# A decoder layer on one core: the routing in groups of 4, 4, 4, 2 and 2 tiles, entered earlier, rows stored by batch

## The reference

```
x = layernorm(x + attn(x))      # linear attention, 16 heads: relu(q), relu(k), kv = k^T v, gated
x = layernorm(x + xattn(x, ctx))
    # q from x, k and v from ctx [8, 256, 512]; 16 heads of 16 rows; softmax over 512 positions
x = layernorm(x + ffn(x))
    logits = x @ router_weight.T + router_bias            # 16 experts
    top_val, top_idx = top_k(logits, 4); top_val = softmax(top_val)
    gate, up = (x @ gate_up_proj[e] + bias)[::2], [1::2]  # gate <= 7, up in -7..7
    out = sum_e score[e] * (((up + 1) * gate * sigmoid(1.702 * gate)) @ down_proj[e] + down_bias[e])
```

## Time and profile before

| | us |
|---|---|
| median of 3 runs (lowest to highest) | 1608.12 (1604.43 to 1608.62) |
| the profiled execution | 1606.24 |
| its span | 1604.6 |
| its mean granted clock | 0.954 |

### The profile page before, as it was taken

The page is one execution under the profiler, slowest core; times in us unless marked ns, Lnnn a source line. Parts: engine busy times, 40 slices in busy tenths (PEclk is TensorE's granted clock), DMA queues, the critical chain, the costliest instruction groups (busy, mean ns, idle before and its releaser), DMA issues. The chain is left out here.

```text
span 1604.6 us, 29621 instructions
## 1 busy us (share of the span) xinstructions
PE 1454.8 (91%) x7542; PEld 1028.6 (64%) x7543; DVE 966.7 (60%) x1414; ACT 738.4 (46%) x1416; POOL 862.1 (54%) x704
## 2 busy tenths in 40 slices
PE   6999999699999999986749999999999999999991
PEld 5878887444444444431537787777777777877770
DVE  2324344778878888898635555555555555555554
ACT  4212222277788778764223444434344443444233
POOL 4425334555666765536146636656666666476221
PEclk9999999799999999998659999999999999999995
DMA  5201022554657556620375545656656566473336
GB/s 215 68 14 49 13 49 54 83 85 72 104 106 130 103 92 121 100 44 19 112 265 128 147 94 158 158 119 154 157 153 157 145 159 158 111 194 74 60 59 219
DMA packets 94741, 180.63 MB, mean 113 GB/s; under 512 B 19113, under 2 KB 21929, under 8 KB 94025
## 3 DMA queue, kind: packets, MB, share of 16 engines
q1 hardware_dynamic: 74968, 133.04, 32.7%
q0 software_dynamic: 18544, 46.13, 14.4%
q10 hardware_dynamic: 1152, 0.52, 0.2%
HBM read 116.32 MB, written 33.73 MB: 94 GB/s over the span
## 5 line engine op out<-in xcount | busy, mean ns | idle before, releaser
L934 DVE TENSOR_REDUCE stage<-ps_a 128x2 f32<-128x1024 f32 x256 | 300.1, 1217 | 70.4 <-PE ps_a L1264 69.8
L1984 POOL TENSOR_TENSOR we_split<-we_raw,we_split 128x512 f32 (+1 forms) x192 | 248.5, 1533 | 108.1 <-ACT we_split L1975 92.8
L734 ACT ACTIVATE probs<-ps_b 128x512 f32<-128x512 f32 x498 | 270.5, 595 | 50.3 <-PE ps_b L1279 44.1
L2288 PE MATMUL ps_y<-we_split,hT 128*128 x912 | 235.4, 407 | 6.0 <-DVE hT L2219 3.5
L2288 PE MATMUL ps_g<-we_split,xT 128*128 x912 | 230.7, 401 | 8.4 <-issue 5.6
L2288 PE MATMUL ps_u<-we_split,xT 128*128 x912 | 231.0, 402 | 0.0
L2288 PEld LDWEIGHTS ps_g<-we_split,xT 128*128 128x128 f32 x912 | 171.1, 190 | 60.4 <-issue 21.3
L2288 PEld LDWEIGHTS ps_y<-we_split,hT 128*128 128x128 f32 x912 | 168.1, 190 | 44.4 <-issue 9.0
L2288 PEld LDWEIGHTS ps_u<-we_split,xT 128*128 128x128 f32 x912 | 166.0, 189 | 34.4
L2087 POOL DMA_INDIRECT scratch_acc<-x_keep,to_rows x76 | 121.2, 1595 | 90.2 <-issue 54.0
L2077 POOL DMA_INDIRECT x_rows<-scratch_x,from_rows x79 | 78.6, 995 | 133.4 <-ACT from_rows L2147 107.7
(11 more groups left out here) (320 smaller groups left out, 2252.7 us busy)
## 6 DMA issues: line engine op xcount, KB each, us to landing
we_raw<-in_w_expert SPq DMA_DIRECT2D x192, 256.0 KB, 2.9
stack<-xT_raw SPq DMA_DIRECT2D x192, 128.0 KB, 5.5
...
scratch_acc<-x_keep SPq DMA_DIRECT2D x1, 4096.0 KB, 18.4
...
```

The lines of the kernel that those rows point to most:

```text
L734: nc.scalar.activation(probs[:, n % 3, h], src[:], ACT.Exp, scale=DH ** -0.5).then_inc(b_kept, 1)
L934: nc.vector.tensor_reduce(out[:, :, i, k % NC], ps_a[i][:], AX.X, ALU.max, negate=True).then_inc(a_kept[i], 1)
L1984: nc.gpsimd.tensor_tensor(lo, W["raw"][:, k, c], hi, ALU.subtract).then_inc(W["lo"], 1)
L2288: mm = nc.tensor.matmul(out[:], left[:, a, c], w[:, bass.ds(par, 1), k, b, c].squeeze(1), start=(n == 0), stop=(n == len(passes) - 1))
```

## The change

The groups are 4, 4, 4, 2 and 2 tiles; `LATE`, the one left for `route()`, has two. Group 0's top_experts, constants and chosen_experts stand in batch 6 at steps 7, 9 and 11. In the last batch stand top 1 (step 0), rank_slots 0 (step 3) and chosen 1 (step 6). Behind the loop VectorE's temporaries lie in ps_a0's second half (`temps_in_psum`), which leaves the ring one bank fewer; rank_slots copies chosen there first. TensorE ranks groups 0, 1, 2 at steps 1, 7, 15 and group 3 behind the last values, has both turns of batch 6 at step 13 and its logits at step 14. GpSimd marks 4 tiles ahead of finish_heads, then 4, then 6. The digits of a slot are compared as integers and two of the three comparisons are one instruction. x is stored to scratch_acc batch by batch behind the store to scratch_x. share_weights of 14 tiles and its store are last. In `route()` the experts' counts and tables are computed around the marks instead of behind them, GpSimd splits gate and up as soon as slots_made has come, the first product waits only for gate, and SP begins with expert 1 once three gathers have landed.

```diff
-                return {3: [("rank", 0)], 4: [("turn", 2 * b - 4)], 5: [("turn", 2 * b - 3), ("rank", 1)],
+                return {1: [("rank", 0)], 4: [("turn", 2 * b - 4)], 5: [("turn", 2 * b - 3)],
...
+                sp.dma_start(S["acc"][b * L:b * L + L, :].rearrange("(i p) d -> p i d", p=P),
+                             x[:, 2 * b:2 * b + 2, :]).then_inc(R["acc_stored"], 16)
...
-                if t == NT - 2:
-                    store_weights(sp, S, R, K["weights"], 0, 3)
+                sp.dma_start(S["acc"][t * P:t * P + P, :], x[:, t, :]).then_inc(R["acc_stored"], 16)
+            store_weights(sp, S, R, K, 0)
...
-                    for t in range(8):
+                    for t in range(4):
...
-            for t in range(8, 10):
-                mark_tile(nc.gpsimd, pool, R, K, t, in_tiles[t], of_tiles[t])
             pool.wait_ge(y2_moments, B - 1)
             nc.gpsimd.tensor_tensor(rstd2[:], mean_var2[:, :, 1], minus_half2[:], ALU.pow).then_inc(y2_rstd, 1)
             for o in range(2):
-                if o == 1:
-                    for t in range(10, EARLY_TILES):
-                        mark_tile(nc.gpsimd, pool, R, K, t, in_tiles[t], of_tiles[t])
+                for t in range(4, 8) if o == 0 else range(8, EARLY_TILES):
+                    if t == 12:
+                        pool.wait_ge(b_made, USE["exp", N - STEPS // 2 - 1, 3] + 1)
+                    mark_tile(nc.gpsimd, pool, R, K, t, in_tiles[t], of_tiles[t])
...
-                if b == B - 1 and s in (0, 2):
-                    if s == 0:
-                        dve.wait_ge(b_made, USE["exp", n - 1, 3] + 1)
-                        dve.wait_ge(b_kept, USE["qk", b, 3, 1] + 1)
-                        dve.wait_ge(v_filled, NC * B)
-                        dve.wait_ge(R["loaded"], 80)
-                        set_choices(nc, dve, R, K)
-                        number_tokens(nc, dve, R)
-                    dve.wait_ge(b_kept, USE["logits", s + 1] + 1)
-                    top_experts(nc, dve, R, K, s // 2, s // 2)
-                if b == B - 1 and s in (1, 3):
-                    chosen_experts(nc, dve, R, K, s // 2, s // 2)
-                if b == B - 1 and s in (5, 6):
-                    dve.wait_ge(b_kept, USE["rank", s - 5] + 1)
-                    rank_slots(nc, dve, R, K, s - 5, s - 5, K["rank"][:, (s - 5) % 2])
+                if b == B - 2 and s == 7:
+                    dve.wait_ge(b_made, USE["qk", B - 1, 3, 1] + 1)
+                    dve.wait_ge(R["loaded"], 80)
+                    dve.wait_ge(b_kept, USE["logits", 1] + 1)
+                    top_experts(nc, dve, R, K, Z, 0)
+                if b == B - 2 and s == 9:
+                    set_ones(nc, dve, R, K)
+                    set_again(nc, dve, R, Z, 4)
+                    number_tokens(nc, dve, R)
+                if b == B - 2 and s == 11:
+                    chosen_experts(nc, dve, R, K, Z, 0, None, R["carry"][:])
+                if b == B - 1 and s == 0:
+                    dve.wait_ge(b_kept, USE["qk", b, 3, 1] + 1)
+                    dve.wait_ge(v_filled, NC * B)
+                    dve.wait_ge(b_made, USE["exp", n - 1, 3] + 1)
+                    dve.wait_ge(b_kept, USE["logits", 3] + 1)
+                    top_experts(nc, dve, R, K, Z, 1)
+                if b == B - 1 and s == 3:
+                    dve.wait_ge(b_kept, USE["rank", 0] + 1)
+                    rank_slots(nc, dve, R, K, Z, 0, K["rank", 0])
+                if b == B - 1 and s == 6:
+                    chosen_experts(nc, dve, R, K, Z, 1, R["carry"][:], R["carry"][:])
+            dve.wait_ge(a_kept[0], N)
+            Z = temps_in_psum(ps_a[0][:, 1], K)
+            fill_temps(nc, dve, R, Z)
+            set_again(nc, dve, R, Z, 4)
+            invert_spread(0)
+            moments(B - 2)
+            dve.wait_ge(b_kept, USE["rank", 1] + 1)
+            rank_slots(nc, dve, R, K, Z, 1, K["rank", 1])
+            dve.wait_ge(y2_rstd, B - 1)
+            for o in range(2):
+                last_norm(B - 2, o, x2_made)
             dve.wait_ge(b_kept, USE["logits", 5] + 1)
-            top_experts(nc, dve, R, K, 2, 2)
-            chosen_experts(nc, dve, R, K, 2, 2)
-            invert_spread(0)
+            top_experts(nc, dve, R, K, Z, 2)
+            chosen_experts(nc, dve, R, K, Z, 2, R["carry"][:], Z["carry"])
             invert_spread(1)
-            moments(B - 2)
             dve.wait_ge(mask_loaded[(B - 1) % 4], 32)
             dve.wait_ge(x2_made, 2 * B - 4)
             add_spread(0)
-            dve.wait_ge(b_kept, USE["rank", 2] + 1)
-            rank_slots(nc, dve, R, K, 2, 2, K["rank"][:, 0])
-            dve.wait_ge(y2_rstd, B - 1)
-            for o in range(2):
-                last_norm(B - 2, o, x2_made)
             dve.wait_ge(x2_made, 2 * B - 2)
             last_moments(0)
+            dve.wait_ge(b_kept, USE["rank", 2] + 1)
+            rank_slots(nc, dve, R, K, Z, 2, K["rank", 2])
             dve.wait_ge(y2_rstd, B)
             last_norm(B - 1, 0, last_step)
+            set_again(nc, dve, R, Z, GROUPS_OF[3][1])
+            dve.wait_ge(b_kept, USE["logits", B - 2] + 1)
+            top_experts(nc, dve, R, K, Z, 3)
+            chosen_experts(nc, dve, R, K, Z, 3, Z["carry"], R["carry"][:])
             invert_spread(2)
-            share_weights(nc, dve, R, K, 0, 3)
+            dve.wait_ge(b_kept, USE["rank", 3] + 1)
+            rank_slots(nc, dve, R, K, Z, 3, K["rank", 3])
             invert_spread(3)
             add_spread(1)
             last_moments(1)
             dve.wait_ge(y2_rstd, B + 1)
             last_norm(B - 1, 1, last_step)
+            share_weights(nc, dve, R, K, range(LATE))
...
-                if s in (4, 5, 14, 15) and b == B - 1:
-                    turn_x2(2 * b - 4 + (4, 5, 14, 15).index(s))
-                if s == 6 and b == B - 1:
-                    logits(b - 2)
-                if s in (3, 5, 11) and b == B - 1:
-                    rank_tokens(nc, pe, R, K, (3, 5, 11).index(s), (3, 5, 11).index(s),
-                                bank("rank", (3, 5, 11).index(s))).then_inc(b_made, 1)
+                if s in (4, 5) and b == B - 1:
+                    turn_x2(2 * b - 4 + (4, 5).index(s))
+                if s == 13 and b == B - 1:
+                    turn_x2(NT - 4)
+                    turn_x2(NT - 3)
+                if s in (6, 14) and b == B - 1:
+                    logits(b - 2 if s == 6 else b - 1)
+                if s in (1, 7, 15) and b == B - 1:
+                    rank_tokens(nc, pe, R, K, (1, 7, 15).index(s), bank("rank", (1, 7, 15).index(s))).then_inc(b_made, 1)
...
             values(N - 1)
+            rank_tokens(nc, pe, R, K, 3, bank("rank", 3)).then_inc(b_made, 1)
             spread_heads(NG * B - 1)
-            logits(B - 2)
+            for t in range(0, 8):
+                spread_tile(nc, pe, R, table, t, in_tiles[t], of_tiles[t])
             turn_x2(NT - 2)
-            for t in range(0, 2):
-                spread_tile(nc, pe, R, table, t, in_tiles[t], of_tiles[t])
             logits(B - 1, (0,))
-            for t in range(2, 9):
+            for t in range(8, EARLY_TILES):
                 spread_tile(nc, pe, R, table, t, in_tiles[t], of_tiles[t])
             turn_x2(NT - 1)
-            for t in range(9, EARLY_TILES):
-                spread_tile(nc, pe, R, table, t, in_tiles[t], of_tiles[t])
             logits(B - 1, (1,))
...
+GROUPS_OF = ((0, 4), (4, 4), (8, 4), (12, 2), (14, 2))
+LATE = len(GROUPS_OF) - 1
+EARLY_TILES = GROUPS_OF[LATE][0]
...
+def temps_in_psum(bank, K):
+
+
+    Z, at = {"top_i": K["top_i"], "picked": K["picked"], "digit": K["digit"]}, 0
+    for name, size in TEMPS[:4] + (("iota", E_), ("b", E_), ("carry", E_)):
+        Z[name] = bank[:, at:at + size]
+        at += size
+    Z["chosen"], Z["mid"] = bank[:, D - 256:D], bank[:, D - 256:D - 128]
+    return Z
+
+
+def fill_temps(nc, dve, R, Z):
+    nc.vector.tensor_copy(Z["iota"], R["iota_f"][:, 0:E_])
+    chain(R, dve, nc.vector.tensor_copy(Z["b"], R["b"][:]))
...
-            sp.dma_start(S["acc"][0:TOK, :].rearrange("(t p) d -> p t d", p=P), x[:]).then_inc(acc_stored, 16)
...
-            store_weights(sp, S, R, K["weights"], LATE, 1)
-
+            store_weights(sp, S, R, K, 1)
             sp.wait_ge(dummy_stored, 32)
-            sp.wait_ge(acc_stored, 16)
             sp.wait_ge(R["weights_stored"], 32)
...
-            pool.wait_ge(R["marked"], 2 * NT)
-            split_lo(nc, pool, W, 0, 0, 0, range(KC))
+            pool.wait_ge(R["slots_made"], LATE + 1)
+            for k in range(2):
+                split_lo(nc, pool, W, 0, 0, k, range(KC))
...
+            for j in range(3):
+                sp.wait_ge(gathered[j], 16)
             load_weights(sp, A, W, 1)
             for e in range(2, E_):
...
-            for k in (UP, DOWN):
-                split_lo(nc, pool, W, 0, 0, k, range(KC))
+            split_lo(nc, pool, W, 0, 0, DOWN, range(KC))
...
```

(6 more changed lines are left out.)

368 lines of the change are left out of this document (205 added, 163 removed).

## The result

| | us, median (range, runs) | ratio to the kernel before, 95% |
|---|---|---|
| before | 1608.37 (1604.43 to 1608.87, 4) | |
| changed | 1588.72 (1588.24 to 1591.02, 4) | 0.9886 [0.9867, 0.9904] |
| changed, again | 1589.34 (1586.43 to 1592.77, 5) | 0.9886 [0.9871, 0.9900] |

The forecast was 1590 us. By the ratio the change is 18.3 us of 1608. First the stages of the changed kernel, to be laid beside the earlier trace rows; the columns are the same.

What follows compares the result with a forecast made beforehand. In 695 to 831 us VectorE, TensorE, a 12.5 us wait for x_keep, TensorE again, then route's DMA were taken to bound. -5.5 - 9.7 - 1.5 + 0 = -16.7 us from 1606.2 gives 1589.5; forecast 1590, range 1578 to 1600.

Steps and rivals of the forecast that it cites:

- 1, insertions: Group 0's choice moved into the batch before, where TensorE bounds: VectorE's inserted pieces cost +4.5 us (bounds 1 and 8).
- 2, first half of the batch: Last batch: VectorE's last reduction ends 31.5 us after the batch's first reduction (u 31.5), not 38.
- 3, the 12.5 us: TensorE's wait for x_keep of batch 6 goes: x_keep at u 43.7, turn at u 45.4, cover under 2 us.
- 4, the tail: Behind the last reduction: new TensorE wait of 5 to 6 us; route starts at u 86.5; with the insertions -5.5 us.
- rival A: Fast tail: TensorE stays at 2.4 GHz from u 31 to the end, 1584.5 us; chance 0.2.
- 5, route: Route without the 4 MB acc store: GpSimd's split is last, barrier 18.9 us after route's start, -9.7 us.
- 6, experts: From barrier to the experts' first product, which waits for gate alone: -1.5 us (bounds -1.1 and -2.5).
- 7, stores by batch: Five 512 KB stores of acc in SP's queue within the loop: taken as 0 us, ends 0 and +3.

Runs made afterwards that it cites:

- r2: The kernel before with only the stores of acc by batch, no 4 MB store in route: 1599.91 us (0.9959).
- g0: The changed kernel with group 0's choice back in the last batch, all at step 0: 1591.74 us (0.9907).
- m1: The changed kernel with GpSimd's marks of tiles 4 to 7 ahead of its rstd of batch 6: 1596.62 us (0.9929).
- t2: The changed kernel with the ranks of group 2 at step 14, ahead of the logits, not at step 15: 1584.80 us (0.9853).
- t4: t2 with one reciprocal for each pair of heads' spreads, two of 128x512 instead of four of 64x512: 1580.47 us (0.9839).
- t5: t4 with route's bias loads behind the small stores and only the gate split by GpSimd ahead of the barrier: 1575.38 us (0.9807).

## Why the forecast came out, point by point

*1, insertions: mis-sized.* Some 2 us, not 4.5. I had stretched them as beside the marks of the earlier trace rows. They did stand beside GpSimd, but beside its scaling of v, and weren't stretched: top_experts took 1.5 us at 669.87, chosen_experts 1.7 at 683.30, while GpSimd ran these:

```profile
669.35 1.85 POOL L519 TENSOR_SCALAR v_aug<-k_sb,stage 128x256 f32<-128x256 f32 x2
...
683.24 2.19 POOL L519 TENSOR_SCALAR v_aug<-k_sb,stage 128x256 f32<-128x256 f32 x2
```

and VectorE the compare, both inputs in SBUF:

```profile
683.30 0.42 DVE L1763 TENSOR_TENSOR stage<-iota_f,stage 128x256 f32<-128x256 f32 x1
```

The same compare takes 0.42 us at 722.66 beside an idle GpSimd, so VectorE lost nothing. GpSimd did: its two operations took 2.19 or 2.20 us in the eleven traces with the compare beside them and 1.84 in the three without it (the kernel before, r2, g0). By the rule of the Trainium skill cited under "Temporaries in PSUM" this pair contends as well, since GpSimd reads SBUF, and the rows agree; here it was GpSimd that paid, 0.35 us.

*2, first half of the batch: right.* Last reduction ends at u 32.4, forecast 31.5; the other traces of this half have 29.5 to 34.1.

*3, the 12.5 us: right.* finish_heads ends at u 33.7, x_keep is done at u 45.2, the turn at u 48.2 doesn't wait. m1 shows the part of the marks.

*4, the tail: right in its waits and its low clock, 4.8 us short, so without the gain I gave it.* The wait is 6.2 us, forecast 5 to 6, but everything is later: 0.9 at the last reduction, 1.9 more by the turn of batch 6, 1.0 more by rank 2 (spread_heads waited 0.7 us for VectorE and ran at the low clock, 3.34 us), 1.2 more in VectorE's last choice (x_keep took 1.38 us beside marks, not 0.6); then it stays: route starts at u 91.3, not 86.5. From the last reduction on I had 55.0 us against 58.5 before, and got 58.9. Together with part 1 I had -5.5 us and got -3.1. That the tail would be at the low clock held (0.57); at its first 32 matmuls rival A's clock came in t2, t4 and t5, with the wait shortened or gone.

*5, route: right*, 18.4 us against 18.9, and bound by GpSimd's split, though the queue ended only 0.4 us sooner. *6, experts: right*, -1.4 against -1.5. *7, stores by batch: right*, 0 as far as the times can tell.

The forecast sum was -16.7 us and the profiled executions differ by 15.2: the start of the last batch came 2.3 better than forecast (0.4 of its 2.2 us was drift before the insertions), the tail 4.7 worse, route and experts 0.2 better, and 0.7 us better lies behind the first product, which wasn't forecast. Two mis-sized terms cancelled by half, which is luck. So is part of the hit on the median: 1590 stood 18.1 us below the 1608.1 of that time, more than the sum of 16.7 gives, and the medians moved by more than the profiled pair.
